# Edge loop of a graph attention layer: attributes staged once a batch, and the row scan, columns and second scans half a step later

## What is computed

```python
x_l = x @ W_l.T + b_l; x_r = x @ W_r.T + b_r; e_feat = e_attr @ W_e.T
s = leaky_relu(x_l[src] + x_r[dst] + e_feat, 0.2)
alpha = einsum('ehc,hc->eh', s, att)
amax = segment_max(alpha, dst)
ex = exp(alpha - amax[dst]); denom = segment_sum(ex, dst)
out = segment_sum((ex / denom[dst])[..., None] * x_l[src], dst) + bias
```

## Time and profile before

| | us |
|---|---|
| device time, median of 3 runs | 3459.81 (3458.88 to 3461.9) |
| span of the profiled execution | 3452.9 |
| of it up to 110, ahead of the edge loop | 110 |
| edge loop, 110 to 1560 | 1450 |
| end of the graph attention, 1560 to 1650 | 90 |
| mixer and experts, 1650 to the end | 1803 |

### The profile page before, as it was taken

One profiled execution on the slowest core, in us unless ns is written; L12 is line 12 of the kernel. 1 busy time (PEld: TensorE's weight loads), 2 busy tenths in 40 slices (PEclk: granted clock), 3 DMA queues, 4 the chain that ended last, 5 costly groups with the idle time before them and its releaser, 6 DMA issues. The chain is left out here.

```text
span 3452.9 us, 50836 instructions
## 1 busy us (share of the span) xinstructions
PE 3048.3 (88%) x13612; PEld 2420.6 (70%) x13613; DVE 1834.2 (53%) x3643; ACT 1508.7 (44%) x4936; POOL 1189.9 (34%) x1152
## 2 busy tenths in 40 slices
PE   6678888788888888884999999999999999999999
PEld 5456656566565665563778877877787888888898
DVE  5566666666676666676754564374365435111103
ACT  2067666777667676775322322232231212222232
POOL 4556555565555655630310031030021001222210
PEclk9899899999999999997999999999999988999999
DMA  7556655555665655554211011100001032333361
GB/s 217 152 148 148 145 145 141 143 144 141 149 145 145 147 142 150 136 94 124 52 38 37 27 30 31 41 8 1 15 27 50 1 100 84 128 120 119 119 176 38
DMA packets 288628, 345.06 MB, mean 100 GB/s; under 512 B 155176, under 2 KB 213655, under 8 KB 284512
## 3 DMA queue, kind: packets, MB, share of 16 engines
q1 hardware_dynamic: 232813, 174.79, 19.1%
q0 software_dynamic: 53632, 157.89, 17.6%
q10 hardware_dynamic: 2064, 10.81, 1.0%
HBM read 298.03 MB, written 44.37 MB: 99 GB/s over the span
## 5 line engine op out<-in xcount | busy, mean ns | idle before, releaser
L1470 POOL DMA_INDIRECT a_g<-xl_d,a_ix x480 | 468.1, 975 | 311.6 <-issue 116.0
L1504 PE MATMUL b_pM<-b_m,b_oh 128*112 128x281 f32 x1680 | 513.6, 451 | 28.5 <-DVE g_acc L1644 22.5
L1599 ACT ACTIVATE b_m<-a_g,c_pcx 128x64 f32<-128x64 f32 x1856 | 460.4, 334 | 33.6 <-issue 33.6
L1504 PEld LDWEIGHTS b_pM<-b_m,b_oh 128*112 128x112 f32 x1680 | 327.6, 200 | 156.7 <-issue 69.0
L1470 POOL DMA_INDIRECT XS<-xl_d,a_ix x344 | 333.3, 969 | 216.5 <-issue 91.1
L1637 DVE SCALAR_TENSOR_TENSOR a_r<-a_pS,g_attx 128x528 f32<-128x528 f32 x420 | 286.6, 699 | 198.4 <-remote 91.6
L1599 ACT ACTIVATE b_m<-XS,c_pcx 128x64 f32<-128x64 f32 x1424 | 351.5, 333 | 14.3 <-issue 14.2
L2286 ACT ACTIVATE f_hid<-f_pH,f_b 128x256 f32<-128x256 f32 (+3 forms) x360 | 161.9, 451 | 423.0 <-PE f_pH L2180 409.9
L450 PE MATMUL m_pH<-m_h,m_w 128*128 128x313 f32 (+1 forms) x1280 | 342.3, 426 | 4.5 <-DVE m_h L612 4.5
L125 POOL TENSOR_TENSOR m_rstd<-m_ve,m_mhalf 125x5 f32<-125x5 f32 x41 | 48.0, 1170 | 801.5 <-DVE m_ve L111 801.5
L1497 PE MATMUL a_pS<-g_xr,a_lt 128*128 x840 | 237.1, 406 | 97.8 <-ACT a_pS L1581 60.8
(11 more groups left out here) (413 smaller groups left out, 4629.2 us busy)
## 6 DMA issues: line engine op xcount, KB each, us to landing
a_db<-dl_d SPq DMA_DIRECT2D x212, 224.0 KB
f_w<-in_ffn_W1p SPq DMA_DIRECT2D x16, 1024.0 KB
wide_w<-in_ffn_W1p SPq DMA_DIRECT2D x16, 1024.0 KB
m_w<-in_mix_W SPq DMA_DIRECT2D x8, 1024.0 KB
f_w<-in_ffn_W2p SPq DMA_DIRECT2D x8, 1024.0 KB
a_g<-xl_d,a_ix POOLq DMA_INDIRECT x480
...
```

The costliest lines, as they stand in the source:

```text
L1470: p.indirect_dma_start(out=gathered(t)[:, j, :], out_offset=None, in_=xl_d, in_offset=bass.IndirectOffsetOnAxis(ap=IX[:, t // BSTEPS, n:n ...
L1504: ins = pe.matmul(pM[0:WN, h, 0:MW], OH[:, b, j, :], M[:, b, j, :], start=(j == 2 * h), stop=(j == 2 * h + 1))
L1599: ins = a.activation(m[:, j, part], gathered(ts)[:, j, part], ACT.Copy, scale=of[:, first + j, h, 0:1])
```

## The change

Attributes: one input tensor `gnn_eab` holds both layouts of a tile side by side (16 KB a row), and one DRAM tensor `eab_d` takes the place of `eat_d` and `ea_d`. Staging is done once a batch: SP loads 28 tile numbers at steps 0 and 7, POOL issues one gather of 28 rows of 16 KB at its steps 2 and 9, and SP stores it with one DMA of 448 KB at steps 5 and 12. Ahead of the loop one gather and one store of 128 rows stand for two each.

Chain: DVE's row scan (before L1721) goes from the end of its slot at tau 0 to its slot at tau 1, behind the one-hot and ahead of the reduce. PE's columns (before L1532) go from ahead of the sums to behind them at tau 1. DVE's second scans and their maximum (before L1702 to L1706, L1726) go from tau 1 to tau 2, between the gates, and the difference (before L1682) goes from there to behind the one-hot. PE's new maximum (before L1558) goes from the end of tau 2 to tau 3, ahead of the transposes back. ACT's instructions stay where they are: its exponential stands at the end of tau 2 and its weighing is in the same steps. The core of the diff (the lines that only rename tensors or sizes are left out):

```diff
 
-                    def staged(i):
-                        at = RI * i + 2 * RI
-                        return slice(at, at + RI) if isinstance(at, int) else bass.ds(at, RI)
+                    def staged(i, t):
+                        at = RI * i + 2 * RI + BI * (t // BSTEPS)
+                        return slice(at, at + BI) if isinstance(at, int) else bass.ds(at, BI)
 
                     def slot(i, base, t):
-                        if exists(base, t, 0) and t == TILES_AT:
-                            wait(sp, "s_gathered", 32 * i, 0)
-                            sp.dma_start(TIX[:, :], tl_d[staged(i)].unsqueeze(1)).then_inc(s["s_tiles"], 16)
-                        elif exists(base, t, 0) and t == STORE_AT:
-                            sp.wait_ge(s["s_gathered"], 32 * i + 32)
-                            sp.dma_start(eat_d[staged(i), :], STG[:, 0, :]).then_inc(s["s_staged"], 16)
-                            sp.dma_start(ea_d[staged(i), :], STG[:, 1, :]).then_inc(s["s_staged"], 16)
+                        if exists(base, t, 0) and t % BSTEPS == TILES_AT:
+                            wait(sp, "s_gathered", 32 * i, 16 * (t // BSTEPS))
+                            sp.dma_start(TIX[:, :], tl_d[staged(i, t)].unsqueeze(1)).then_inc(s["s_tiles"], 16)
+                        elif exists(base, t, 0) and t % BSTEPS == STORE_AT:
+                            sp.wait_ge(s["s_gathered"], 32 * i + 16 * (t // BSTEPS) + 16)
+                            sp.dma_start(eab_d[staged(i, t), :], STG[:, :]).then_inc(s["s_staged"], 16)
                         elif exists(base, t, 0) and t == RING - attributes_ahead:
                             wait(sp, "s_staged", 32 * i, 0)
...
-                        if t == GATHER_AT:
-                            p.wait_ge(s["s_tiles"], 16 * i + 16)
-                            wait(p, "s_staged", 32 * i, 0)
+                        if t % BSTEPS == GATHER_AT:
+                            p.wait_ge(s["s_tiles"], 32 * i + 16 * (t // BSTEPS) + 16)
+                            wait(p, "s_staged", 32 * i, 16 * (t // BSTEPS))
                             p.sem_inc(s["a_seen"], 1)
-                            for n, a in enumerate((g["eaT"], g["ea"])):
-                                p.indirect_dma_start(out=STG[:, n, :], out_offset=None, in_=a,
-                                                     in_offset=bass.IndirectOffsetOnAxis(ap=TIX[:, 0:1], axis=0)).then_inc(s["s_gathered"], 16)
+                            p.indirect_dma_start(out=STG[:, :], out_offset=None, in_=g["eab"],
+                                                 in_offset=bass.IndirectOffsetOnAxis(ap=TIX[:, 0:1], axis=0)).then_inc(s["s_gathered"], 16)
...
                         elif tau == 3:
+                            pe.wait_ge(s["c_diff"], n)
+                            pe.matmul(pA[0:1, 0:GH], FB[:, 0, 0:1], by_item(ident[0:CP, 0:CP])[:, :, 0], start=True, stop=True).then_inc(s["c_new"], 1)
                             pe.wait_ge(s["c_p"], n)
                             pe.wait_ge(s["c_cl"], n)
                             for d in range(2):
...
-                        if tau == 1:
-                            pe.wait_ge(s["c_rowscan"], n)
-                            for d in range(2):
-                                ins = pe.matmul(pY[0:CP, 240 + d:241 + d], ST[0:1, par, d, d:d + CP], one[:, :], start=True, stop=True)
-                            ins.then_inc(s["c_cols"], 1)
...
-                        if tau == 2:
-                            pe.wait_ge(s["c_diff"], n)
-                            pe.matmul(pA[0:1, 0:GH], FB[:, 0, 0:1], by_item(ident[0:CP, 0:CP])[:, :, 0], start=True, stop=True).then_inc(s["c_new"], 1)
+                        if tau == 1:
+                            pe.wait_ge(s["c_rowscan"], n)
+                            for d in range(2):
+                                ins = pe.matmul(pY[0:CP, 240 + d:241 + d], ST[0:1, par, d, d:d + CP], one[:, :], start=True, stop=True)
+                            ins.then_inc(s["c_cols"], 1)
...
                         elif tau == 2:
-                            v.wait_ge(s["c_max"], n)
-                            v.tensor_tensor(FB[:, 1, :], scores, FB[:, 0, :], ALU.subtract).then_inc(s["c_diff"], 1)
+                            v.wait_ge(s["c_cols"], n)
+                            v.tensor_copy(IN[:, :], pY[0:CP, 240:242]).then_inc(s["c_init"], 1)
+                            v.wait_ge(s["c_init"], n)
+                            v.sem_inc(s["c_seen"], 1)
+                            v.tensor_tensor_scan(FB[:, 0, :], BR[:, par, 0, :], scores, IN[:, 0:1], ALU.add, ALU.max)
+                            v.tensor_tensor_scan(FB[:, 1, ::-1], BR[:, par, 1, ::-1], scores[:, ::-1], IN[:, 1:2], ALU.add, ALU.max).then_inc(s["c_rescan"], 1)
+                            v.wait_ge(s["c_rescan"], n)
+                            v.tensor_tensor(FB[:, 0, :], FB[:, 0, :], FB[:, 1, :], ALU.max).then_inc(s["c_max"], 1)
...
                         if tau == 1:
-                            v.wait_ge(s["c_cols"], n)
-                            v.tensor_copy(IN[:, :], pY[0:CP, 240:242]).then_inc(s["c_init"], 1)
-                            v.wait_ge(s["c_init"], n)
-                            v.sem_inc(s["c_seen"], 1)
-                            v.tensor_tensor_scan(FB[:, 0, :], BR[:, par, 0, :], scores, IN[:, 0:1], ALU.add, ALU.max)
-                            v.tensor_tensor_scan(FB[:, 1, ::-1], BR[:, par, 1, ::-1], scores[:, ::-1], IN[:, 1:2], ALU.add, ALU.max).then_inc(s["c_rescan"], 1)
+                            v.wait_ge(s["c_rows"], n)
+                            for d, way in enumerate((1, -1)):
+                                ins = v.tensor_tensor_scan(ST[0:1, par, d, 0:CP][:, ::way], ANY[0:1, par, d, :, :].rearrange("p h i -> p (h i)")[:, ::way],
+                                                           pY[0:1, d * CP:(d + 1) * CP][:, ::way], LOW, ALU.add, ALU.max)
+                            ins.then_inc(s["c_rowscan"], 1)
...
                         elif tau == 2:
+                            v.wait_ge(s["c_max"], n)
+                            v.tensor_tensor(FB[:, 1, :], scores, FB[:, 0, :], ALU.subtract).then_inc(s["c_diff"], 1)
...
-                        if tau == 0:
-                            v.wait_ge(s["c_rows"], n)
-                            for d, way in enumerate((1, -1)):
-                                ins = v.tensor_tensor_scan(ST[0:1, par, d, 0:CP][:, ::way], ANY[0:1, par, d, :, :].rearrange("p h i -> p (h i)")[:, ::way],
-                                                           pY[0:1, d * CP:(d + 1) * CP][:, ::way], LOW, ALU.add, ALU.max)
-                            ins.then_inc(s["c_rowscan"], 1)
-                        elif tau == 1:
-                            v.wait_ge(s["c_rescan"], n)
-                            v.tensor_tensor(FB[:, 0, :], FB[:, 0, :], FB[:, 1, :], ALU.max).then_inc(s["c_max"], 1)
```

29 lines of the change are left out of this document (13 added, 16 removed).

## The result

The changed kernel takes 3488.97 us (median of 4 runs, 3484.44 to 3494.98) against 3460.86 for the kernel before (4 runs, 3458.88 to 3463.84): a ratio of 1.0079 (1.0061 to 1.0096), 28 us slower. The forecast was 3452, 9 us faster; 3488.97 lies above the range of 3415 to 3485.

What follows compares the result with a forecast made beforehand. It took the edge loop as bound by engines waiting for each other, in stops ending by POOL's last gather. Terms of -10.5 + 3 + 0 = -7.5 us gave 3452 us, with 3415 to 3485 for 8 in 10.

Steps and rivals of the forecast that it cites:

- The common end of the stops: Edge loop: engines' shared waits end together, about 2 us behind POOL's last gather; removing the row scan's wait leaves ACT's.
- rival D: Edge loop: stops end by POOL's gathers, waits of equal length refill PE's restart, nothing moves: 3460 us; chance 0.13.
- Part 1: Row scan and columns leave the restart after a stop: 0.35 us a batch, 10.5 us gained.
- rival A: PE's sums after a stop: higher clock or sums done inside the stop, about 3420 us (3405 to 3440); chance 0.22.
- Part 2: Second scans between step 2's gates: mostly hidden by waits, 0.1 us a batch, 3 us lost.
- rival B: Step 2 becomes the bound: late second gate, exponential and ACT's copy, 3480 us (range 3470 to 3495); chance 0.18.
- Rival C: Odd stop grows by POOL's whole delay from late tile numbers: 24 to 30 us, 3470 (3465 to 3480); chance 0.12.
- Part 3: PE's new maximum moved to step 3, ahead of the transposes back: no cost and no gain.
- Part 4: Staging once a batch, POOL waiting for tile numbers 30 times instead of 15: 0, range -6 to +16 us.
- Odd and even stops: Stops of a ring's two batches: staging once a batch makes them nearly equal in length.
- The rule on PE's end: PE's recorded end is an estimate; semaphores await PSUM's acknowledgement, so DVE waiting for another PE semaphore gains nothing.
- The rule on packets: DMA queues shared by staging and row gathers: uncut 16 KB rows hold an engine twice as long as 8 KB rows.

Runs made afterwards that it cites:

- e4: Kernel before with the ring's tile numbers loaded at step 2, staging gathers at step 5, stores at step 8: 3458.82 us, ratio 0.9996, with the stops.
- e2: Kernel before with the change's chain alone, staging as it was: 3476.10 us, ratio 1.0050, on a chip with the stops.
- e17: Kernel before with the chain alone, PE also loading step 2's window numbers ahead of its wait for the row scan: ratio 1.0042, without the stops.
- e14: Kernel before with the change's chain alone, run again on a chip without the stops: ratio 1.0056.
- e5: Kernel before with the chain alone, but the difference right behind the maximum, between the gates of step 2: ratio 1.0052, without the stops.
- e7: Kernel before with the chain alone, but ACT's exponential behind its copy of step 3: ratio 1.0059, without the stops.
- e6: Kernel before with only second scans, maximum and difference between step 2's gates, new maximum at the end of step 2: ratio 1.0027, without the stops.
- e1: Kernel before with the change's staging alone, chain where it was: 3470.64 us, ratio 1.0036, on a chip with the stops.
- e11: Kernel before, unchanged, traced on a chip without the stops: its loop takes 1106.8 us in place of 1373.3.
- e9: Kernel before with one staging gather of 56 rows of 16 KB and one store a ring: ratio 0.9951, without the stops.

## Why the prediction was wrong, point by point

**The common end of the stops held in the main, where there are stops.** The wait of the row scan is gone, those of the adds and the gates took it over, and ACT's stayed (207.1 for 180.9). e4 shows it once more. Held to the letter it isn't right, as the add that came free at 831.83 shows. The prediction drew the right conclusion from it only for rival D, and then booked a gain of 0.35 us a batch all the same.

**Part 1 failed: 10.5 us of gain, with the clock taken to stay as it is.** The chain, parts 1 to 3, was to gain 7.5 us in all and lost 17 (e2). Three things stand in place of the gain.

First, the restart. Where a stop caught PE at its sums they started again 0.66 us behind the end (the median of 21 idle times of over 1.5 us in after), as part 1 said. But 11 such idle times end at L1540, 1.92 us behind, and five at the transposes L1514, 2.46 us behind: the stop had moved on to where PE needs DVE's scans or reduce. PE's time without work didn't fall but grew, by 10.1 us in after and by 13.8 in e2.

Second, the columns. They were to "cost PE 0.56 to 0.93 us there", and without the stops they cost 1.26 us, since a wait as the last thing of PE's slot lays the register load of the next slot bare. e17 shows this cause, there and for the batches in which step 2 doesn't wait for rows. With the stops PE has the same wait (17.6 us in 29 times in after, 18.3 in 32 in e2), and it is near the 17 us that the chain lost, but that is no proof: e4 has 24.8 us of it in 31 times and loses nothing. The closing paragraph named the place ("if the wait of the columns for the row scan, now behind the sums, holds PE for more than 1 us a batch") but looked for a wait for DVE, and PE hardly waits for that (PE 2.1 us in all of after). I counted matmuls and semaphores, and not the instructions that issue nothing on the engine.

Third, the clock. Part 1 took it "to stay as it is", and rival A had it only as a gain. In e2 PE's matmuls took 15.3 us more, in after 16.9, in e14 15.1 and in e17 11.5. By the estimate above the lower clock is all of this in e14 and e17, most of it in e2 (12.8 us), and under half of it in after (7.5 us); what the rest is stays open.

**Part 2 was about right, without the stops.** 0.1 us a batch was said, and e17 shows 36.11 against 36.04 where step 2 isn't started from a standstill. The chain of rival B came as written: gate, one-hot, difference, exponential, copy, with ACT's exponential waiting 87.5 us. Without the stops e5 and e7 took that lateness away and gained nothing. With them no run tried it, so that rival B, whose range of 3470 to 3495 holds the measured time, is not excluded there.

**Two slips in the sums.** Rival C's 24 to 30 us, less what the other parts gave, lead from 3460 to some 3473 to 3483, and not to 3470. The forecast's own range stands as 3445 to 3459 in one sentence and 3440 to 3462 in another. Neither moves the forecast.

**Part 3 held, and for a reason that I didn't see.** Left at the end of step 2, the new maximum becomes the same bare load, 22.0 us in e6. In after it stands inside a slot.

**Part 4's forecast of 0 failed too; its range was right and its mechanism wrong.** -6 to +16 was said, e1 measured +12. POOL waited for tile numbers no longer than before (3 waits in after over 200 to 1400, where 30 a run were said), so rival C's mechanism isn't it. PE's idle time didn't grow either. What grew is the time of its matmuls, by 23.6 us in the trace of e1, 21 of them at the lower clock by the estimate above. Why a gather in both batches brings more of the lower clock with the stops is open; without them the same kernel gains 18 us and has no more of it than before. e4 says that for a staging once a ring the step at which it comes is free with the stops. The gather at step 4, or one a ring, was not tried there.

**Odd and even stops.** They were to become nearly equal. Before, batches alternate, 45.5 and 50.0 us; in after they are irregular, 44 to 53.5 behind the first, with no order. The medians of the two kinds are 48.7 and 47.9, so this much came true, and by the staging, as part 4 had it: they are 47.8 and 48.9 in e1, and 44.3 and 53.4 in e2.

**The rule on PE's end** was cited for the 9.3 us between a matmul's recorded end and its waiter's start. The Trainium skill (Perfetto Trace Analysis, the lifecycle of a Tensor engine instruction) puts the acknowledgement of PSUM between the two. e11 shows that the same pair takes under a microsecond on another chip, where the scan starts at 485.51 behind a reduce that ends at 485.58; so that rule alone doesn't give the length of a stop.

**The rule on packets** (the Trainium skill, DMA: Bandwidth & Descriptors, Queues, rings and completion order) would have had rows of 16 KB, if they are not cut, hold up others. e9 against before shows no harm: 0.9951 with them.
